# New waits for the late blocks' statistics and matmuls in the last search, and new preferences for the order of the queues

## The chip, the cores and the metric

The kernel runs on one core of a Trainium2 chip. The metric is the time of one execution on the device, in microseconds (us), and the number compared is the median of several runs.

## The reference

Two batches of 4096 tokens with 256 channels go through causal single-head attention and through a routed feed-forward layer. Each is followed by a residual sum and a normalisation. In the feed-forward layer the 3072 tokens of each batch with the highest router score get `x + gelu(x @ w_block)`. The others get `x + x`.

```python
x = _layernorm(x + attn(x, w_attn, b_attn, w_proj, b_proj))   # causal softmax(q k^T / 16) v, then w_proj
scores = jnp.einsum('bld,d->bl', x, w_router)
_, top_idx = jax.lax.top_k(scores, k)                          # k = 3072 of 4096, per batch
selected = jnp.take_along_axis(x, top_idx[:, :, None], axis=1)
processed = jax.nn.gelu(jnp.einsum('bkd,de->bke', selected, w_block))
out = x.at[batch_idx, top_idx].set(processed)
x = _layernorm(x + out)
```

## The kernel before, in words

**Groups.** The 8192 queries are cut into 16 groups of 512, eight for each batch (G = 0 to 15). For a group the kernel first projects queries and values. It casts a block of the transposed x to its high part (`xhi`, ScalarE, L747) and subtracts that for the low part (`xlo`, GpSimd, L765). TensorE then makes two query halves in bank fbank, which `qhi` (ScalarE, L792) and `qlo` (VectorE, L797) turn into high and low parts. The values are made in the same way (`vhi`, L826, and `vlo`, L830), and SyncE stores them in DRAM (L841). From there they are loaded again for every group that needs them, into six buffers (L1019).

**Attention.** Scores are matmuls into sbank (line L515 of the helper `split3`), tile by tile, 128 keys by 512 queries. ScalarE copies them to a ring (L872), VectorE keeps a running maximum, subtracts it (L982), ScalarE takes the exponential and a high part (L989, L996), VectorE the low part (L1001), and TensorE multiplies with the values (L1049 to L1051). The output is normalised, the router score is taken, and the feed-forward part follows: a transposition (L1340), matmuls, gelu (L1392), a sum on GpSimd (L1404), statistics `bn_stats` on VectorE (L1410) and their means `bn_aggr` (L1415). GpSimd makes the final scale factors from those (`final_roots`).

**Two late groups.** The feed-forward part of groups 14 and 15 (`LATE` is 14) is done after the last attention matmul, in single-pass matmuls (L1374), one piece for each half group j and 128-token tile.

**The search.** Which tokens are left out follows from a search for the 3072nd highest score. It has eight rounds (`ROUNDS` is 4, two halves of the key). In each round VectorE compares all keys with 15 thresholds (L1503, in two pieces for the second batch), TensorE counts the hits (L1559), and VectorE reduces the counts and decides (L1514, L1520). Between the counts TensorE gets fillers without use for the result (L555). After the last round come the ties (L1526, L1527, L1575, L1577) and the selection (L1534 to L1539). For the second batch, VectorE then picks one of two ready outcomes for 256 tokens at a time (L1752, 16 picks), and SyncE stores each pick (L1715).

**What sets the order.** The order of every queue is computed before the program is built. Each piece of work belongs to a named stream of an engine. The planner (`planned`, called by `merged`) rehearses all streams with costs of its own and takes for each engine the piece that can start first. `MARGIN_US` makes a stream's pieces look later, and `PREFER_US` lets them win where several could start. Among pieces that could start at one time the longest remaining way decides, to which the preference is added. Waits that a piece carries count in the rehearsal, so an added wait moves its piece. Each engine then works strictly in that order. On the chip a piece waits at its turn for its semaphores, and all that stands behind it in its queue waits too.

The semaphores of the change are `p_last` (counts of the second search done, by TensorE), `v_cmp` (compares done), `v_sel` (tie masks made) and `v_tie` (tie positions made), all three by VectorE.

Of the kernel before, what the change touches and what calls it, by code (L numbers as in the profile page):

```python
# [17 lines left out]
B, T, C = 2, 4096, 256  # L18
# [3 lines left out]
QT = GQ // P  # L22
# [12 lines left out]
ROUNDS = 4  # L35
# [7 lines left out]
LATE = 2 * (T // GQ) - 2  # L43
# [9 lines left out]
COLD_US, COLD, COLD_STREAMS = 4.0, 1.85, ()  # L53
TABLE_US = 1.28

PREFER_US = {"ffn flo": 100, "final load": 100, "project vhi": 100, "ffn store": 100, "last chain": 60,
             "last router": 60, "project qhi": 60, "attention_out residual": 60, "project qlo": 60,
             "attention_out stats": 60, "ffn fhi": 60, "attention_out score": 60, "row_max": 60,
             "final store": 60, "search first": 60, "scores copy": 30, "softmax hi": 30, "final pick": 30,
             "search": 30, "ffn stats": 15, "values load": 15, "prepare xlo": 8, "attention_out norm": 8,  # L60
             "row_max reduce": 4, "project xhi": 4, "project vlo": 4, "softmax lo": 4, "ffn gelu": 4,
             "project load": 4, "attention_out evac": 4, "prepare bias": 4, "scores hide": -4, "softmax exp": -4,
             "softmax z": -4, "final result": -4, "ffn add": -4, "ffn aggr": -8, "attention_out router": -8,
             "attention_out aggr": -8, "attention_out istd": -8, "last": -8, "final scale": -15, "final own": -15,
             "final choose": -30, "prepare": -30}
MARGIN_US = {"attention_out router": 3, "final scale": 3, "project xhi": 2, "ffn flo": 2, "final_roots": 2,
             "prepare bias": 1.5, "out": 1.5, "ffn store": 1.5, "scores hide": 1, "values load": 0.6,
             "ffn aggr": 0.6, "row_max reduce": 0.6, "values": 0.6, "project load": 0.3, "proj": 0.3,
             "attention_out stats": 0.3}

COSTS = {"pe": (.0, 1 / 2400, .2), "act": (.13, 1 / 1200, .14), "dve": (.09, 1 / 960, .12),
# [208 lines left out]
def program(nc, x, xt, w_attn_t, columns, w_proj, b_proj, w_router, w_block, out):  # L280

    gid = lambda b, g: b * NG + g
    groups = [(b, g) for b in range(B) for g in range(NG)]
# [39 lines left out]
    for f in out_fills:  # L323
        kind, G, j = f
# [4 lines left out]
    for f in late_fills:  # L329
        kind, G, j = f  # L330
# [12 lines left out]
    with ctx:  # L343
# [59 lines left out]
        score = sb("score", [P, B, NT])  # L403
# [42 lines left out]
        p_s, p_proj, p_out, p_last, p_late = sem("p_s"), sem("p_proj"), sem("p_out"), sem("p_last"), sem("p_late")  # L446
# [11 lines left out]
        v_cnt, v_tie, v_srch, v_cmp, v_sel = sem("v_cnt"), sem("v_tie"), sem("v_srch"), sem("v_cmp"), sem("v_sel")  # L458
# [12 lines left out]
        def bank_of(f):  # L471
            return (fbank + sbank + obank)[bank_no[f]]
# [85 lines left out]
        def late_busy(pe):  # L558

            pe.wait_ge(v_h, QT * len(groups))  # L560
            busy(pe, fbank[2][:, :], 2)
# [764 lines left out]
        def ffn(G):  # L1326

            b, g = groups[G]
            late = G >= LATE
# [27 lines left out]
                                  ALU.subtract).then_inc(v_flo, 1)  # L1357

            def pe_f(pe, j, tiles_=(0, 1)):
                if late and 0 in tiles_:  # L1360

                    pe.wait_ge(v_rs, 2 * len(groups) - 1)
                if late and 0 in tiles_:
                    pe.wait_ge(a_fhi, 2 * G + j + 1)
                    pe.wait_ge(ld_late, 16)
                    freed(pe, ("ff", G, j))
                elif 0 in tiles_:
                    pe.wait_ge(v_flo, 2 * G + j + 1)
                    if G == 0:
                        pe.wait_ge(v_wb, 2)  # L1370
                    freed(pe, ("ff", G, j))
                for t in tiles_ if late else ():
                    for k in range(CC):
                        mm = pe.matmul(bank_of(("ff", G, j))[:, t * C:(t + 1) * C],  # L1374
                                       x1p_of(G, j)[:, 0, k * 2 * P + t * P:k * 2 * P + (t + 1) * P], late_wb[:, k],
                                       start=k == 0, stop=k == CC - 1)
                for t in () if late else tiles_:
                    mm = split3(pe, bank_of(("ff", G, j))[:, t * C:(t + 1) * C],
                                lambda h, k: x1p_of(G, j)[:, h, k * 2 * P + t * P:k * 2 * P + (t + 1) * P],
                                lambda h, k: WB[:, h, k, :], CC)  # L1380
                if 1 in tiles_:
                    mm.then_inc(p_late if late else p_out, 1)
                    if G == LATE and j:
                        late_busy(pe)
# [14 lines left out]
            def add(pool, j):  # L1399
# [3 lines left out]
                    pool.wait_ge(v_sc, 2 * len(groups))  # L1403
                pool.tensor_tensor(y_pair(G, j), x1_pair(G, j), y_pair(G, j), ALU.add).then_inc(g_y, 1)  # L1404

            def stats(dve, t):
                dve.wait_ge(g_y, 2 * G + t // 2 + 1)
                if G and t == 0:
                    dve.wait_ge(v_mvy, QT * G)
                dve.bn_stats(bnst[:, 1, t, :], y_pair(G, t // 2)[:, t % 2]).then_inc(v_bny, 1)  # L1410

            def aggr(dve):
                for t in range(QT):
                    dve.wait_ge(v_bny, G * QT + t + 1)
                    dve.bn_aggr(mv_y[:, b, g * QT + t, :], bnst[:, 1, t, :]).then_inc(v_mvy, 1)  # L1415
# [475 lines left out]
```

## Time and profile before

| | |
|---|---|
| median of 3 runs | 969.17 us (966.97 to 973.5) |
| the profiled execution: its time | 968.08 us |
| the profiled execution: its span | 966.4 us |
| TensorE busy | 97% of the span |
| VectorE busy | 80% |
| ScalarE busy | 66% |
| mean granted clock of TensorE | 0.989 |
| last attention matmul (L1051) starts | 925.66 us |
| first pick starts | 951.42 us |

The times in the profile count from the span's start. The execution's own time is 1.68 us longer than the span. Line numbers are those of the kernel before.

### The profile page before, as it was taken

How to read it: one execution, taken by the hardware profiler on the slowest of the kernel's cores; microseconds unless marked ns; L12 is line 12 of the kernel's file. 1: busy time of each engine (PE TensorE's matmuls, PEld its weight loads, DVE VectorE, ACT ScalarE, POOL GpSimd, SP SyncE). 2: the span in 40 equal slices, each digit the busy share in tenths (PEclk: the TensorE clock that was granted, in tenths of full speed). 3: DMA queues.
4: the chain of work that ended last, by engine and by line, in shares of the span. 5: the costliest groups of instructions: out<-in, count | busy, mean ns of one | idle time of the engine just before them, and what ended most of it. 6: DMA issues, size and time to landing. Idle time of an engine off the chain costs nothing.

```text
span 966.4 us, 15640 instructions
## 1 busy us (share of the span) xinstructions
PE 939.0 (97%) x5078; PEld 805.6 (83%) x5078; DVE 769.3 (80%) x1473; ACT 635.3 (66%) x993; POOL 273.4 (28%) x436
## 2 busy tenths in 40 slices
PE   9999999999999999999999999999999999998991
PEld 7889988888888888888888999888888888887770
DVE  5688996967966786689769999887898778569977
ACT  3566675764864585478555875686688558447985
POOL 3523124253052034512214243323204302211162
PEclk9999999999999999999999999999999999999996
DMA  6535343344253345567433533535778534437935
GB/s 191 175 122 167 115 143 120 120 131 139 80 164 99 102 150 163 157 224 223 155 113 93 194 114 105 164 97 179 243 234 243 178 103 130 120 100 232 314 119 174
DMA packets 89378, 149.53 MB, mean 155 GB/s; under 512 B 7761, under 2 KB 25810, under 8 KB 89298
## 3 DMA queue, kind: packets, MB, share of 16 engines
q1 hardware_dynamic: 89298, 148.54, 48.9%
q8 instruction: 41, 0.67, 0.3%
q14 instruction: 39, 0.32, 0.1%
HBM read 108.66 MB, written 39.85 MB: 154 GB/s over the span
## 4 chain that ended last, share of the span: by engine, by line
PE 94%; DVE 3%; issue 1%; ACT 1%; POOL 0%; ACTq 0%; DVEq 0%; POOLq 0%
PE sbank L515 37%; PE fbank L515 13%; PE obank L1049 11%; PE obank L1051 11%; PE obank L1050 11%; PE obank L1043 2%; PE obank L1045 2%; PE obank L1044 2%; PE fbank L1340 1%; PE fbank L1139 1%; PE mbank L947 1%; PE mbank L970 1%; DVE cmp L1503 1%; PE obank L555 1%; ACT parts L996 0%
## 5 line engine op out<-in xcount | busy, mean ns | idle before, releaser
L515 PE MATMUL sbank<-qT,xT 128*128 128x512 f32 (+2 forms) x1728 | 413.2, 379 | 0.0
L515 PEld LDWEIGHTS sbank<-qT,xT 128*128 128x128 f32 x1728 | 306.4, 189 | 53.0 <-issue 0.3
L872 ACT COPY ring<-sbank 128x512 f32<-128x512 f32 (+3 forms) x288 | 157.6, 549 | 178.2 <-PE sbank L515 126.9
L1001 DVE TENSOR_TENSOR ring_lo<-ring,parts 128x1024 fp32r<-128x1024 f32 (+4 forms) x176 | 179.6, 1027 | 30.9 <-ACT parts L996 30.2
L1049 PE MATMUL obank<-ring_lo,vs 128*128 128x512 f32 x480 | 183.6, 383 | 4.3 <-ACT parts L996 2.6
L1051 PE MATMUL obank<-parts,vs 128*128 128x512 f32 x480 | 181.9, 379 | 0.0
L1050 PE MATMUL obank<-parts,vs 128*128 128x512 f32 x480 | 181.6, 378 | 0.0
L996 ACT CAST parts<-ring 128x1024 fp32r<-128x1024 f32 (+4 forms) x176 | 145.9, 834 | 51.7 <-PE obank L1051 38.9
L982 DVE TENSOR_TENSOR ring<-ring,mbank 128x1024 f32<-128x1024 f32 (+4 forms) x176 | 159.4, 946 | 9.4 <-PE mbank L970 9.4
L989 ACT ACTIVATE ring<-ring 128x1024 f32<-128x1024 f32 (+4 forms) x176 | 143.9, 844 | 24.7 <-DVE ring L982 24.4
L914 DVE TENSOR_TENSOR runmax<-ring,runmax 128x1024 f32<-128x1024 f32 x84 | 107.2, 1276 | 64.7 <-ACT ring L872 64.1
L1404 POOL TENSOR_TENSOR yb<-xres,yb 128x512 f32<-128x512 f32 x28 | 38.4, 1393 | 249.8 <-ACT yb L1392 249.8
L1049 PEld LDWEIGHTS obank<-ring_lo,vs 128*128 128x128 f32 x480 | 90.3, 188 | 20.8 <-ACT parts L996 3.3
L1051 PEld LDWEIGHTS obank<-parts,vs 128*128 128x128 f32 x480 | 90.2, 188 | 17.0
L1050 PEld LDWEIGHTS obank<-parts,vs 128*128 128x128 f32 x480 | 90.4, 188 | 15.9
L1100 POOL TENSOR_TENSOR xres<-xres,b_tot 128x512 f32<-128x512 f32 x32 | 50.9, 1610 | 66.9 <-DMA xres<-x 65.6
L909 DVE TENSOR_TENSOR runmax<-ring,runmax 128x512 f32<-128x512 f32 (+3 forms) x76 | 42.6, 561 | 15.6 <-ACT ring L872 14.2
L765 POOL TENSOR_TENSOR xT<-xraw,xT 128x512 fp32r<-128x512 f32 x27 | 35.2, 1324 | 66.9 <-ACT xT L747 65.9
L1070 POOL TENSOR_SCALAR roots<-mv_h 128x4 f32<-128x4 f32 x15 | 5.3, 357 | 163.2 <-DVE mv_h L1168 148.5
L515 PE MATMUL fbank<-WV,xT 128*128 128x256 f32 x384 | 51.1, 283 | 0.0
L515 PEld LDWEIGHTS fbank<-WV,xT 128*128 128x128 f32 x384 | 49.5, 191 | 1.7
L515 PE MATMUL fbank<-xT,A 128*128 128x512 f32 x192 | 49.3, 393 | 1.6 <-DVE qT L797 0.8
(222 smaller groups left out, 1203.6 us busy)
## 6 DMA issues: line engine op xcount, KB each, us to landing
vs<-v_scratch SPq DMA_DIRECT2D x288, 256.0 KB, 2.8
v_scratch<-vnew SPq DMA_DIRECT2D x30, 512.0 KB, 3.2
xres<-x SPq DMA_DIRECT2D x16, 512.0 KB, 4.6
out<-tail SPq DMA_DIRECT2D x32, 256.0 KB, 3.2
x_scratch<-xres SPq DMA_DIRECT2D x14, 512.0 KB, 3.0
y_scratch<-yb SPq DMA_DIRECT2D x14, 512.0 KB, 4.6
tail<-x_scratch SPq DMA_DIRECT2D x28, 256.0 KB, 3.5
tail<-y_scratch SPq DMA_DIRECT2D x28, 256.0 KB, 4.3
```

The costliest lines, as they stand in the source:

```text
L515: mm = eng.matmul(o, lhs(lh, k), rhs(rh, k), start=n == 0, stop=n == len(todo) - 1)
L872: act.copy(slot(n)[:, c0:], sbank[n % NSS][:, c0:]).then_inc(a_copy, 1)
L909: dve.tensor_tensor(runmax[:, 0, c0:], slot(n)[:, c0:], runmax[:, 0, c0:], ALU.max).then_inc(v_max, 1)
L914: dve.tensor_tensor(runmax[:, :, :], slots(ns, 0), runmax[:, :, :], ALU.max).then_inc(v_max, 1)
L982: dve.tensor_tensor(slots(ns, c0), slots(ns, c0), mbank[:, None, c0:].broadcast_to([P, len(ns), GQ - c0]), ALU.subtract).then_inc(v_z, 1)
L989: act.activation(slots(ns, c0), slots(ns, c0), ACT.Exp, scale=SCALE).then_inc(a_exp, 1)
L996: act.copy(hi_of(u), slots(ns, c0)).then_inc(a_hi, 1)
L1001: dve.tensor_tensor(slots_lo(ns, c0), slots(ns, c0), f32(hi_of(u)), ALU.subtract).then_inc(v_lo, 1)
L1049: pe.matmul(o, vh, lo_, start=i == 0, stop=False)
L1050: pe.matmul(o, vh, hi_, start=False, stop=False)
L1051: mm = pe.matmul(o, vl, hi_, start=False, stop=last)
L1100: pool.tensor_tensor(r[:, 2 * j:2 * j + 2], r[:, 2 * j:2 * j + 2], b_tot[:, None, :].broadcast_to([P, 2, C]), ALU.add).then_inc(g_xres, 1)
```

## The change

It has three parts.

1. The tables `PREFER_US` and `MARGIN_US` have other entries: `project vhi` (100), `final pick` (60) and `softmax exp` (-4) go, `attention_out store` (30) comes, `project xhi` goes from 4 to 15 and loses its margin of 2, `search first` goes from 60 to 30, and a few more.
2. Each late matmul piece of group 15 (`pe_f`) waits for a number of counts: 2 for half 0 tile 0, then 3, 4 and 5.
3. Each statistic of groups 14 and 15, and the means of each, gets a place in the search by a wait (`late_turn`). The numbers n run from 0 to 4 for group 14 and from 5 to 9 for group 15. Up to 6 the wait is for the compares of a round, 7 waits for the tie masks, and 8 and 9 wait for the tie positions.

```diff
+             "values load": 15, "project xhi": 15, "prepare xlo": 8, "attention_out norm": 8, "ffn gelu": 8,
...
             def pe_f(pe, j, tiles_=(0, 1)):
+                if G == len(groups) - 1:
+
+                    pe.wait_ge(p_last, 2 + 2 * j + tiles_[0])
                 if late and 0 in tiles_:
...
+            def late_turn(dve, t):
+
+                n = (G - LATE) * (QT + 1) + t
+                if n < 2 * ROUNDS - 1:
+                    dve.wait_ge(v_cmp, 2 * ROUNDS + 2 * (n + 2))
+                elif n == 2 * ROUNDS - 1:
+                    dve.wait_ge(v_sel, 2 * B)
+                else:
+                    dve.wait_ge(v_tie, B)
+
             def stats(dve, t):
                 dve.wait_ge(g_y, 2 * G + t // 2 + 1)
+                if late:
+                    late_turn(dve, t)
...
             def aggr(dve):
+                if late:
+                    late_turn(dve, QT)
```

The order of all five queues follows from this anew. The tables of the order below show three places. Names are those of the tiles, with the buffer's number; the words in brackets are the semaphores that an instruction waits for. In the order of the change the lines have other numbers (L746 is L747 of before, L791 is L792).

ScalarE at the start, before: two casts of the first x block, the two query halves, then two casts of the next x blocks.

```order
L750 CAST xT<-xraw 128x512 [waits ld_xh0]
L750 CAST xT<-xraw 128x512 [waits ld_xh1]
L792 ACTIVATE qT<-fbank0,ucol 128x512 [waits v_u,p_proj]
L792 ACTIVATE qT<-fbank1,ucol 128x512 [waits v_u,p_proj]
L747 CAST xT<-ring 128x2x512 [waits ld_xt0_1]
L747 CAST xT<-ring 128x2x512 [waits ld_xt0_2]
```

The same place with the change:

```order
L749 CAST xT<-xraw 128x512 [waits ld_xh0]
L749 CAST xT<-xraw 128x512 [waits ld_xh1]
L791 ACTIVATE qT<-fbank0,ucol 128x512 [waits v_u,p_proj]
L746 CAST xT<-ring 128x2x512 [waits ld_xt0_1]
L791 ACTIVATE qT<-fbank1,ucol 128x512 [waits v_u,p_proj]
L746 CAST xT<-ring 128x2x512 [waits ld_xt0_2]
```

The first of the two casts now stands between the two query halves.

TensorE in the third and fourth round of the last search, before (cmp is what is counted, obank0 takes group 15's late matmuls, fbank2 the fillers):

```order
L1374 MATMUL obank0<-runmax,late_x 128x256 [waits ld_late,a_fhi,v_rs]
L1374 MATMUL obank0<-runmax,late_x 128x256
L1559 MATMUL fbank0<-cmp,ones_bf 128x120 [waits v_cnt,v_cmp]
L1559 MATMUL fbank0<-cmp,ones_bf 128x120
L1374 MATMUL obank0<-runmax,late_x 128x256 x2
L1559 MATMUL fbank0<-cmp,ones_bf 128x120 [waits v_cmp]
L1559 MATMUL fbank0<-cmp,ones_bf 128x120
L555 MATMUL fbank2<-ones_bf 128x512 [waits v_h]
L555 MATMUL fbank2<-ones_bf 128x512
L1340 MATMUL obank1<-ident,tail 128x128 [waits v_ot,v_ow,p_last,a_x1]
```

The same place with the change (L1376 is L1374 of before, L1575 is L1559):

```order
L1376 MATMUL obank0<-runmax,late_x 128x256 [waits ld_late,a_fhi,v_rs,p_last]
L1376 MATMUL obank0<-runmax,late_x 128x256
L1575 MATMUL fbank0<-cmp,ones_bf 128x120 [waits v_cnt,v_cmp]
L1575 MATMUL fbank0<-cmp,ones_bf 128x120
L1575 MATMUL fbank0<-cmp,ones_bf 128x120 [waits v_cmp]
L1575 MATMUL fbank0<-cmp,ones_bf 128x120
L554 MATMUL fbank2<-ones_bf 128x512 [waits v_h]
L554 MATMUL fbank2<-ones_bf 128x512
L1376 MATMUL obank0<-runmax,late_x 128x256 [waits p_last]
L1376 MATMUL obank0<-runmax,late_x 128x256
L1339 MATMUL obank1<-ident,tail 128x128 [waits v_ot,v_ow,p_last,a_x1]
```

The second pair of late matmuls has moved from between the count's two pieces to behind the count and its filler. The last four (sbank0) are parted in the same way: two stay ahead of the fifth count, and two go ahead of the sixth.

VectorE from the last decision of the search to the end, before:

```order
L1526 TENSOR_SCALAR gteq<-mbank,tab 128x32 [waits v_srch]
L1527 TENSOR_SCALAR gteq<-mbank,tab 128x32
L1415 BN_AGGR mv_y<-bnst 128x2 [waits v_bny] x4
L1534 SCALAR_TENSOR_TENSOR keyf<-ones,fbank 128x64 [waits p_last]
L1535 TENSOR_TENSOR keyf<-keyf,fbank 128x32 [waits v_srch]
L1537 SCALAR_TENSOR_TENSOR keyf<-keyf,gteq 128x32 [waits v_tie]
L1539 SCALAR_TENSOR_TENSOR mbank<-keyf,gteq 128x32 [waits v_srch]
L1752 COPY_PREDICATED tail<-mbank,tail 128x512 [waits a_own,a_sums,v_srch]
L1752 COPY_PREDICATED tail<-mbank,tail 128x512 [waits a_sums,a_own,v_srch] x15
```

The same place with the change:

```order
L1542 TENSOR_SCALAR gteq<-mbank,tab 128x32 [waits v_srch]
L1543 TENSOR_SCALAR gteq<-mbank,tab 128x32
L1424 BN_STATS bnst<-tail 128x6 [waits v_sel,g_y]
L1550 SCALAR_TENSOR_TENSOR keyf<-ones,fbank 128x64 [waits p_last]
L1551 TENSOR_TENSOR keyf<-keyf,fbank 128x32 [waits v_srch]
L1553 SCALAR_TENSOR_TENSOR keyf<-keyf,gteq 128x32 [waits v_tie]
L1555 SCALAR_TENSOR_TENSOR mbank<-keyf,gteq 128x32 [waits v_srch]
L1424 BN_STATS bnst<-tail 128x6 [waits v_tie,g_y,v_srch]
L1768 COPY_PREDICATED tail<-mbank,tail 128x512 [waits a_sums,a_own,v_srch] x5
L1431 BN_AGGR mv_y<-bnst 128x2 [waits v_bny,v_tie]
L1431 BN_AGGR mv_y<-bnst 128x2 [waits v_bny] x3
L1768 COPY_PREDICATED tail<-mbank,tail 128x512 [waits a_sums,a_own,v_srch] x11
```

Two statistics now stand behind the search's last compare, and the means stand behind the fifth pick. In the rounds before, the statistics are one after the third compare, two after the fourth, one after the fifth, the means after the sixth, and one each after the seventh and eighth. Before they are two after the third and two after the fourth, the means and one after the fifth, one after the sixth, none after the seventh and two after the eighth.

## Rows read from the trace of the kernel before

**Rows 1.** The page, part 1: busy us, share of the span and instructions.

```profile
PE 939.0 (97%) x5078; PEld 805.6 (83%) x5078; DVE 769.3 (80%) x1473; ACT 635.3 (66%) x993; POOL 273.4 (28%) x436
```

**Rows 2.** TensorE's waits, whole span: who waited for whom, us in total, times, longest.

```profile
PE obank L1049 <- ACT parts L996: 2.6, 2, 1.4
...
PE fbank L515 <- DVE qT L797: 0.8, 1, 0.8
```

**Rows 3.** Busy us of PE, PEld, DVE, ACT, POOL; PE clock, DMA share, GB/s.

```profile
500.00:600.00 100.00, 99.71 (x654) 90.90 (x653) 92.62 (x221) 70.27 (x118) 37.94 (x69) 1.00 0.42 134
```

**Rows 4.** Timeline, 0 to 36 us: start, us, engine, line, out<-in, idle time before.

```profile
11.93 0.69 ACT L792 ACTIVATE qT<-fbank,ucol 128x512 fp32r<-128x512 f32 x1 [0.67 <-PE fbank L515]
12.65 0.75 DVE L797 SCALAR_TENSOR_TENSOR qT<-fbank,ucol,qT 128x512 fp32r<-128x512 f32 x1 [0.61 <-ACT qT L792]
...
13.31 0.42 DVE L692 CAST WB<-ring 128x512 fp32r<-128x512 f32 x1
...
14.68 1.05 ACT L747 CAST xT<-ring 128x1024 fp32r<-128x1024 f32 x1 [2.07 <-DMA ring<-xt]
...
15.80 2.70 POOL L765 TENSOR_TENSOR xT<-ring,xT 128x512 fp32r<-128x512 f32 x2 [8.01 <-ACT xT L747]
15.81 1.55 DVE L677 CAST WV<-ring 128x512 fp32r<-128x512 f32 x1
...
16.37 4.26 PE L515 MATMUL sbank<-qT,xT 128*128 128x512 f32 x12
17.40 1.65 DVE L681 TENSOR_TENSOR WV<-ring,WV 128x512 fp32r<-128x512 f32 x1
...
20.47 3.04 PE L515 MATMUL fbank<-WV,xT 128*128 128x256 f32 x24
```

**Rows 5.** Busy time in single microseconds at the start, columns as in rows 3.

```profile
16.00:17.00 1.00, 1.00 (x4) 0.63 (x4) 1.00 (x1) 0.95 (x1) 1.00 (x1) 0.85 1.09 352
...
20.00:21.00 1.00, 1.00 (x9) 1.00 (x8) 0.43 (x1) 0.33 (x1) 0.00 (x0) 0.94 0.08 16
```

**Rows 6.** The chain that ended last, 920 us on: start, us, what.

```profile
936.78 0.43 PE fbank L555 x2
937.22 0.86 PE obank L1374 x4
938.18 0.92 PE obank L1374 x4
939.25 0.30 DVE mbank L1514
...
940.64 0.66 DVE bnst L1410 x2
...
945.35 0.30 DVE mbank L1514
...
947.11 0.30 DVE mbank L1514
...
948.50 0.66 DVE bnst L1410 x2
...
950.01 0.29 DVE mv_y L1415 x4
```

**Rows 7.** Timeline of the end, and the busy time of one microsecond of it.

```profile
951.42 9.85 DVE L1752 COPY_PREDICATED tail<-mbank,tail 128x512 f32<-128x512 uint32 x16
...
953.38 2.08 ACT L1742 ACTIVATE tail<-tail,fin 128x256 f32<-128x256 f32 x4 [1.47 <-POOL fin L1643]
...
964.00:965.00 1.00, 0.00 (x0) 0.00 (x0) 0.00 (x0) 0.00 (x0) 0.00 (x0) 0.50 1.02 348
```

**Rows 8.** SyncE's waits, and the page's part 6 on value loads.

```profile
SPq L1019 <- PE obank L1051: 431.5, 197, 7.9
...
SPq L841 <- DVE vnew L830: 65.0, 23, 10.9
...
vs<-v_scratch SPq DMA_DIRECT2D x288, 256.0 KB, 2.8
```

More of the change, by code:

```diff
@@ L54 @@
 TABLE_US = 1.28
[L56 to L65, printed above, removed]
@@ L66 @@
-MARGIN_US = {"attention_out router": 3, "final scale": 3, "project xhi": 2, "ffn flo": 2, "final_roots": 2,
+PREFER_US = {"ffn flo": 100, "final load": 100, "ffn store": 100, "last chain": 60, "last router": 60,
+             "project qhi": 60, "attention_out residual": 60, "project qlo": 60, "attention_out stats": 60,
+             "ffn fhi": 60, "attention_out score": 60, "row_max": 60, "final store": 60, "scores copy": 30,
+             "softmax hi": 30, "search": 30, "search first": 30, "attention_out store": 30, "ffn stats": 15,
+             "values load": 15, "project xhi": 15, "prepare xlo": 8, "attention_out norm": 8, "ffn gelu": 8,
+             "row_max reduce": 4, "project vlo": 4, "softmax lo": 4, "project load": 4, "attention_out evac": 4,
+             "prepare bias": 4, "scores hide": -4, "softmax z": -4, "final result": -4, "ffn add": -4,
+             "attention_out router": -8, "attention_out aggr": -8, "attention_out istd": -8, "last": -8,
+             "final scale": -15, "final own": -15, "final_roots own": -15, "final choose": -30, "prepare": -30}
@@ L67 @@
+MARGIN_US = {"attention_out router": 3, "final scale": 3, "last": 3, "ffn flo": 2, "final_roots": 2,
              "prepare bias": 1.5, "out": 1.5, "ffn store": 1.5, "scores hide": 1, "values load": 0.6,
-             "ffn aggr": 0.6, "row_max reduce": 0.6, "values": 0.6, "project load": 0.3, "proj": 0.3,
+             "row_max reduce": 0.6, "values": 0.6, "ffn aggr": 0.3, "project load": 0.3, "proj": 0.3,
              "attention_out stats": 0.3}
```

## The prediction

> **What bounds the kernel now.** I read the page's busy times first: TensorE is busy 939.0 of 966.4 us [rows 1]. What it waited for in the whole span comes next: softmax parts 2.6 us, a query's low part 0.8 us, and less than that for each of the rest but three [rows 2]. So until the last block TensorE decides alone, and a change of order on the other engines is worth at most those waits, or costs what it adds to them. The middle is where the others are fullest: VectorE is busy 92.62 us of 500 to 600, TensorE still 99.71 [rows 3]. Two places are different. At the start all engines are strung on one chain of loads, casts and matmuls [rows 4, 5]. At the end TensorE's array is nearly idle, the chain goes through VectorE's compares, counts and statistics [rows 6], and then through 16 picks and 16 stores [rows 7].
>
> The profiled execution took 968.08 us, 1.68 more than its span, and lies 1.09 under the median of the runs shown, 969.17. I make the sum against 968.08 and add 1.09 for the median.
>
> **Start: ScalarE's cast of the second x block before the second query half.** The changed tables put this cast (L747) ahead of the second query evacuation (L792). Before, that evacuation starts at 11.93 and takes 0.69, VectorE's low part follows at 12.65, and the cast starts at 14.68, after 2.07 us of waiting for its load [rows 4]. The load's own start hangs on other loads alone, so its landing should not move. ScalarE works in order: it will stand at the cast until 14.68, end it at 15.73, and evacuate the query half by 16.42. VectorE's low part takes 0.75: to 17.20. The first scores need it. They now start at 16.37 (16.44 on the chain), right behind other matmuls; they will start at 17.25, and that is +0.8 us of idle TensorE that nothing hides.
>
> Queued behind that low part on VectorE are the casts of the block's weights (from 13.31) and all of the value weights (15.81 to 19.05) [rows 4]. 17.13 takes the place of 13.31, so the value weights' cast comes 3.8 us later, at 19.6, with one 0.15 us column moved ahead of it at 19.8. Those two instructions take 1.55 and 1.65 now, beside GpSimd's subtraction, which runs from 15.80 to 18.50. The same form of cast at 13.31, with GpSimd idle, took 0.42. By 19.8 GpSimd is done, so I count 0.42 and, for the low part, the 0.75 of the query's: ready at 20.9. But now the cast that began at 13.31 starts inside GpSimd's 15.80 to 18.50, and pays the difference of 1.55 and 0.42: ready at 22.0. The scores themselves run 4.1 us, mostly at the lower clock, so they end at about 21.4. The value projection, which starts at 20.47 now, waits for the later of both. Bounds: +0.8 (only the scores count) and +1.5 (VectorE's chain). I take +1.4, since the cast meets the very GpSimd instruction that the 1.55 us row met.
>
> The clock in this stretch: 0.85 granted from 16 to 17 and 0.94 from 20 to 21 [rows 5], so the lower level, 1.2 GHz, from about 16.7 to 20.1; before it fell TensorE was busy all the time. I let the low stretch move with the scores.
>
> Two rules speak here. The Trainium skill, "SBUF — State Buffer", "Who interferes with whom", makes the port that VectorE shares with GpSimd an exclusive lock, held for a whole instruction. By it the cast at 17.13 does nothing until 18.50 and ends at 18.92, and the start costs 1.6 instead of 1.4. The Trainium skill, "TensorE: Matmul & The Clock Gate", Part 1, says that the monitor behind the clock runs free and is not set off by the program. By it the clock could return at 20.1 all the same, the scores would end 0.2 us earlier, and the sum stays, as VectorE's chain is later.
>
> **Body: orders of all engines re-dealt.** Some forty single matmul groups change places on TensorE, and ScalarE's and VectorE's orders differ in the first 130 us, at 345 to 450 and at 470 to 720. From about 830 to 930 no engine's order differs, so the waits there (the 2.6 of [rows 2] among them) stay. Of the moved places only two show a TensorE wait of now: 0.8 for a query's low part at 422 and 0.3 for a running maximum at 523. Gain at most 1.1. On the other side, moves of one or two ScalarE instructions (about 1 us each) where VectorE is 93% busy [rows 3] can open new waits of 0.3 to 1.5 us, as the existing ones are. I take 0, and keep -1.1 and +3.
>
> **Last block: search, late matmuls, statistics.** A round of the search that nothing disturbs takes 1.76 us from one count's reduce to the next (945.35 to 947.11) [rows 6].
> - Third count: two late matmul groups of 0.86 and 0.92 stand around its first piece, and its reduce comes at 939.25, 2.43 after the one before. The change puts the second of them behind the whole count: 0.67 earlier.
> - Fourth count: that group, the transposes and two fillers (0.43 each) now stand ahead of it. From 938.5: 0.43 + 0.9 + 0.45 + 0.43 and the count's 0.35 give a reduce at 941.05. Now it comes at 941.2, held by two statistics (0.66). So 0.5 of the 0.67 is given back; 0.15 stays.
> - Fifth: means (0.29, as for the ties) and one statistic (0.33, half of a pair) after the compare become one statistic, and only half of the eight late matmuls is ahead of the count: 0.35 earlier.
> - Sixth and seventh: means or one statistic (0.3 to 0.4) fit under the count, which takes that long after the compare: 0.
> - Eighth: two statistics (0.66, ending at 949.16) become one; the reduce comes 2.0 after 947.11 instead of 1.76: 0.2 earlier.
> - Ties: a statistic instead of the means (0.29) under TensorE's two matmuls: 0.
> - The new waits on v_cmp, v_sel and v_tie are for instructions that VectorE itself has just ended. Each costs the overlap of two neighbours, under 0.1 us, and lies under the count: 0. What stands behind them is the next reduce.
> - The last statistic comes after the selection and before the first pick: 0.4 later.
> Together the first pick moves by -0.7 + 0.4 = -0.3 us, to 951.1.
>
> The picks take 9.85 us for 16, the transfers of 4.19 MB at 348 GB/s take 12.1 [rows 7], so the transfers end the kernel and start with the first pick. The means between the fifth and the sixth pick (0.37) are hidden: after five picks the transfers are 0.7 us behind, and at the end 2.3 us. The last two picks now need, after the means, GpSimd's roots (950.30 to 953.38, 3.1 us) and four ScalarE scalings (2.08) [rows 7]: 951.1 + 5 x 0.62 + 0.4 + 5.1 = 959.7, and the last pick starts at 960.8. The cover is 1.1 us thick here and 2.3 more in the transfers. If the means come over 3 us late, this is the new end. Term: -0.3; bounds -0.8 (the fourth count keeps its gain) and +0.4 (the rounds give nothing).
>
> **Sum.** 968.08 + 1.4 + 0 - 0.3 = 969.2, and 970.3 for the median.
>
> **Rivals.**
> 1. *The rounds give nothing.* If counts are paced by TensorE's late groups in every round, the first pick comes 0.1 to 0.4 later. For it: the fourth count already is. Against: the sixth to eighth have no late group. 968.08 + 1.4 + 0.4 + 1.09 = 971.0. Chance 0.18.
> 2. *Faster.* The x block lands before 12.6 when nothing else waits for it, or the clock's low stretch shrinks, so the start costs nothing; the waits at 422 and 523 go (-1.1); the tail gives 0.8. 968.08 - 1.9 + 1.09 = 967.3. Against: the load's landing is read at 14.68 and its chain of loads is not touched. Chance 0.15.
> 3. *Slower: the value projection loses its preference (100 to 0).* Six of its casts on ScalarE come later (at 346.7 it is passed by about seven instructions, to some 12 us later), then VectorE's part, then the store, and the SyncE queue is in order: the loads of value tiles stand behind that store. For it: the queue already stands 65.0 us for these parts [rows 8]. Against: the loads wait 431.5 us for free buffers, up to 7.9 at a time, and TensorE never for a load [rows 2, 8]. It decides from where a store comes more than the six buffered tiles (8 to 16 us) late; each such place costs up to a landing of 2.8 us [rows 8]. One or two places: +3, 973.3; all six: +17. Chance 0.20, of which 0.04 for over 9.7 us.
> That a wait added is already satisfied, and so changes nothing but the listed order, is part of the forecast: the order is what acts.
> The forecast itself has 0.47.
>
> **Range and chances.** Runs of one kernel spread over 966.97 to 973.5, so a median of a few can move by some 2 us. 966.6 takes in half of rival 2, 974.2 the common part of rival 3. A measurement here can tell about 1%, 9.7 us. Only the far end of rival 3 reaches that, and nothing on the other side but an error of mine: faster 0.02, within 0.94, slower 0.04.
>
> **What would show it.** In the new profile: ScalarE's cast at 14.7 ahead of the second query part, and the first scores at 17.2 (right) or 16.4 (wrong: rival 2). The value projection at 21.4 to 22.2. Reduces of the third and fourth count 1.8 and about 2.45 apart, the eighth 1.8 after the seventh. First pick about 0.3 earlier counted from the last value matmul, five picks, the means, eleven picks without a gap, DMA share at 1.0 to the end. New TensorE waits for value loads would mean rival 3. A difference of over 3 us with none of these would make the whole reading wrong.

## The result and the profile after

The changed kernel takes 974.08 us (median of 13 runs, 971.37 to 976.11), the one before 969.17 (13 runs, 966.97 to 973.5): a ratio of 1.0044, with an interval of 1.0032 to 1.0057. It is slower by some 4 us. The number lies inside the range (966.6 to 974.2) by 0.1 us, and within the 1% that I called the same. The forecast was 1.1 us more, not 4, and the upper end of the range stood for rival 3, which did not happen. So the hit of the range is luck.

The profiled execution has a span of 970.7 us, 4.3 more than before. Lines have moved: L746 is L747 of before, L791 L792, L796 L797, L871 L872, L1424 L1410, L1431 L1415, L1530 L1514, L1768 L1752. Its page, part 1, against [rows 1]:

```profile
PE 940.1 (97%) x5078; PEld 805.5 (83%) x5078; DVE 772.9 (80%) x1473; ACT 634.4 (65%) x993; POOL 275.2 (28%) x436
```

TensorE has 1.1 us more of work and 4.3 us more of span, so most of the loss is waiting. Its waits (us in total, times, longest) against [rows 2]:

```profile
PE obank L1048 <- ACT parts L995: 3.1, 2, 1.7
...
PE mbank L946 <- DVE runmax L908: 1.2, 2, 0.9
PE sbank L514 <- ACT ring L871: 1.2, 1, 1.2
...
PE fbank L514 <- DVE qT L796: 0.8, 1, 0.8
```

Two are new against that profile, 1.2 on the ring's copy and 0.95 on the running maximum. (The second turns up in traces of the old order too, see below.) The wait of 0.8 at the query's low part is still there: a gain at the places that I had allowed to go did not come.

**The start** (start, us, engine, line, out<-in, idle before), against [rows 4]:

```profile
14.56 1.04 ACT L746 CAST xT<-ring 128x1024 fp32r<-128x1024 f32 x1 [3.15 <-DMA ring<-xt]
...
15.51 0.68 ACT L791 ACTIVATE qT<-fbank,ucol 128x512 fp32r<-128x512 f32 x1
15.68 2.76 POOL L764 TENSOR_TENSOR xT<-ring,xT 128x512 fp32r<-128x512 f32 x2 [7.91 <-ACT xT L746]
...
16.23 0.75 DVE L796 SCALAR_TENSOR_TENSOR qT<-fbank,ucol,qT 128x512 fp32r<-128x512 f32 x1 [4.03 <-ACT qT L791]
16.89 0.41 DVE L691 CAST WB<-ring 128x512 fp32r<-128x512 f32 x1
...
17.08 4.21 PE L514 MATMUL sbank<-qT,xT 128*128 128x512 f32 x12 [0.48 <-issue]
17.34 1.65 DVE L693 TENSOR_TENSOR WB<-ring,WB 128x512 fp32r<-128x512 f32 x1
...
20.34 0.43 DVE L676 CAST WV<-ring 128x512 fp32r<-128x512 f32 x1
20.80 0.69 DVE L680 TENSOR_TENSOR WV<-ring,WV 128x512 fp32r<-128x512 f32 x1
...
21.55 0.62 PE L514 MATMUL fbank<-WV,xT 128*128 128x256 f32 x3 [0.27 <-DVE WV L680]
```

The cast stands ahead of the query half, waits for its load and delays the first scores to 17.08 (17.2 was forecast). VectorE's chain of weights ends last, and the value projection starts at 21.55 instead of 20.47. The clock of that stretch, against [rows 5]:

```profile
16.00:17.00 1.00, 0.60 (x2) 0.19 (x2) 0.77 (x2) 1.00 (x2) 1.00 (x2) 1.00 1.09 356
17.00:18.00 1.00, 0.92 (x2) 0.83 (x3) 0.97 (x2) 0.13 (x1) 1.00 (x1) 0.50 1.10 363
20.00:21.00 1.00, 1.00 (x6) 0.96 (x5) 0.93 (x5) 0.59 (x1) 0.00 (x0) 0.79 0.00 0
```

It fell to 1.2 GHz, as in the profile of before, here at the moment when the scores began.

**Where the 4.3 us arise.** Matched by the number of the value matmul, TensorE is behind by 1.08 us from the value projection to 355 us, by 2.46 at 407, by 3.62 at 574 and by 4.27 at 906. After that nothing is lost: the first pick starts 25.86 us after the last attention matmul (25.76 before). The four steps are 1.08, 1.38, 1.16 and 0.6 us. The second is this one, first before (VectorE's means and ScalarE, 399 to 406 us), then after:

```profile
399.10 0.37 DVE L1168 BATCH_NORM_AGGREGATE mv_h<-bnst 128x2 f32<-128x6 f32 x4
402.89 0.59 ACT L872 COPY ring<-sbank 128x512 f32<-128x512 f32 x1 [0.24 <-PE obank L1051]
404.43 1.59 ACT L1250 ACTIVATE xres<-xres,rstd,rs_h 128x256 f32<-128x256 f32 x3 [0.96 <-POOL rstd L1209]
```

```profile
401.19 0.37 DVE L1167 BATCH_NORM_AGGREGATE mv_h<-bnst 128x2 f32<-128x6 f32 x4
401.65 1.05 ACT L995 CAST parts<-ring 128x1024 fp32r<-128x1024 f32 x1
406.57 0.60 ACT L1249 ACTIVATE xres<-xres,rstd,rs_h 128x256 f32<-128x256 f32 x1 [3.86 <-POOL rstd L1208]
407.07 0.56 ACT L871 COPY ring<-sbank 128x512 f32<-128x512 f32 x1
407.69 1.65 PE L514 MATMUL sbank<-qT,xT 128*128 128x512 f32 x6 [1.18 <-ACT ring L871]
```

The new order puts a normalisation ahead of a copy. The normalisation waits 3.86 us for GpSimd's factor, the copy waits behind it, and the scores wait 1.18 us for the bank that the copy frees. VectorE's new order has a part in it: the means from which GpSimd makes that factor start at 401.19 instead of 399.10, 2.1 us later, where TensorE was only 1.0 behind. Near 570 us, the third step, GpSimd's final factors stand ahead of the roots that the normalisations need, and the copies stand behind these:

```profile
570.07 1.09 ACT L1249 ACTIVATE xres<-xres,rstd,rs_h 128x256 f32<-128x256 f32 x2 [1.73 <-POOL rstd L1208]
```

This order is not the whole cause there: three traces of the old order (the waits alone, the end by hand, the new end alone) have a wait of 0.85 to 1.10 us on the same running maximum. The fourth step is a load of x that landed after 6.0 instead of 5.5 us.

**The end** (VectorE), against [rows 6] and the picks of [rows 7]:

```profile
950.91 0.27 DVE L1530 TENSOR_REDUCE mbank<-fbank 128x15 f32<-128x120 f32 x1
...
951.44 0.84 DVE L1519 SCALAR_TENSOR_TENSOR cmp<-mbank,tab,jtab 128x240 bf16<-128x240 f32 x2
952.74 0.43 DVE L1424 BATCH_NORM_STATS2 bnst<-tail 128x6 f32<-128x256 f32 x1 [0.46 <-DVE cmp L1519]
953.08 0.27 DVE L1530 TENSOR_REDUCE mbank<-fbank 128x15 f32<-128x120 f32 x1
...
955.79 3.14 DVE L1768 COPY_PREDICATED tail<-mbank,tail 128x512 f32<-128x512 uint32 x5
958.83 0.36 DVE L1431 BATCH_NORM_AGGREGATE mv_y<-bnst 128x2 f32<-128x6 f32 x4
```

From one reduce to the next, third to eighth: 1.76, 2.37, 2.13, 1.75, 1.81, 2.17 us, and 2.71 to the first pick. Before: 2.43, 1.96, 2.40, 1.74, 1.76, 1.97 and 2.34. In the eighth round VectorE stands idle for 0.46 us between the compare that it has ended and the statistic that waits for this very compare. The picks then run as forecast, and the transfers last to the end as in the last row of [rows 7]:

```profile
968.00:969.00 1.00, 0.00 (x0) 0.00 (x0) 0.00 (x0) 0.00 (x0) 0.00 (x0) 0.50 1.02 341
```

### The profile page after: what moved, and what is told of

The parts are those of the page before. It is cut to its first block, busy times and chain, and to the rows that moved or that the text cites. A ratio compares the mean times of both kernels' runs of the same rounds, so it can differ in the third digit from the quotient of the medians.

```text
span 970.7 us, 15647 instructions
## 1 busy us (share of the span) xinstructions
PE 940.1 (97%) x5078; PEld 805.5 (83%) x5078; DVE 772.9 (80%) x1473; ACT 634.4 (65%) x993; POOL 275.2 (28%) x436
## 4 chain that ended last, share of the span: by engine, by line
PE 81%; DVE 6%; POOL 4%; issue 4%; DMA 3%; ACT 2%; DVEq 0%; SPq 0%; ACTq 0%; POOLq 0%
PE sbank L514 32%; PE fbank L514 12%; PE obank L1048 10%; PE obank L1050 10%; PE obank L1049 10%; DMA xraw<-xt 2%; PE obank L1042 1%; PE obank L1044 1%; PE obank L1043 1%; POOL xT L764 1%; PE fbank L1339 1%; PE mbank L946 1%; PE fbank L1138 1%; PE mbank L969 1%; DVE ring L981 1%
## 5 line engine op out<-in xcount | busy, mean ns | idle before, releaser
L871 ACT COPY ring<-sbank 128x512 f32<-128x512 f32 (+3 forms) x288 | 157.5, 548 | 172.1 <-PE sbank L514 126.6
L1000 DVE TENSOR_TENSOR ring_lo<-ring,parts 128x1024 fp32r<-128x1024 f32 (+4 forms) x176 | 181.6, 1040 | 27.5 <-ACT parts L995 26.3
L913 DVE TENSOR_TENSOR runmax<-ring,runmax 128x1024 f32<-128x1024 f32 x84 | 110.4, 1315 | 66.4 <-ACT ring L871 65.7
L764 POOL TENSOR_TENSOR xT<-xraw,xT 128x512 fp32r<-128x512 f32 x27 | 40.0, 1501 | 56.9 <-ACT xT L746 56.0
```

Of the source, the lines that this page charges most:

```text
L764: pool.tensor_tensor(xT[:, 1, k, cols], raw_of(G)[:, k, :], f32(xT[:, 0, k, cols]), ALU.subtract).then_inc(g_xlo, 1)
L871: act.copy(slot(n)[:, c0:], sbank[n % NSS][:, c0:]).then_inc(a_copy, 1)
L913: dve.tensor_tensor(runmax[:, :, :], slots(ns, 0), runmax[:, :, :], ALU.max).then_inc(v_max, 1)
L1000: dve.tensor_tensor(slots_lo(ns, c0), slots(ns, c0), f32(hi_of(u)), ALU.subtract).then_inc(v_lo, 1)
```

## The experiments

Theory A held that the places of the new order in the start and the body cost the 4 us, theory B that the waits in the search do. Theory C came up on the way: the wait near 570 us differs from one execution to the next, and not by the order. So did theory D: the swap at the start costs much because TensorE stands idle ahead of the first scores and its clock then falls. Orders were put together by overwriting stretches of the planned lists of streams, such as:

```diff
     orders, times = planned(todo, signalled, urgency(todo))
+    for e, at, names in PLACED:
+        orders[e][at:at + len(names)] = names
```

Ratios are to the kernel before, which ran again beside each group of experiments: 29 runs with a median of 970.1 for the first four, 26 with 968.3 for the next four, 32 with 969.38 for the last four. Single traces of one order differ by up to 2 us at the start alone, so I read places from traces and sums from ratios.

### The waits alone, with the old tables

```diff
-PREFER_US, MARGIN_US = (the new tables)
+PREFER_US, MARGIN_US = (the old tables)
```

> The kernel with the change, but with the old tables of preferences and margins: only the waits of the late statistics and of group 15's late matmuls are left. Theory A (the cost comes from three places of the new order: start 1.1 us, near 407 us 1.4, near 572 us 1.2): the last attention matmul starts within 0.3 us of where it does before (925.66), the first pick follows it by 25.8 to 25.9 us instead of 25.76, and the time is 968.7 to 969.7 where before has 969.2, a ratio of 1.000 to 1.001. Theory B (the waits in the search cost it, and the steps before it are scatter of one profiled execution): the ratio stays at 1.004. The eighth count's reduce comes 2.17 us after the seventh, as with the change, if the 0.46 us that VectorE stood ahead of that round's statistic belongs to the order, and 1.8 if it was scatter.

972.2 us, ratio 1.0018 (1.0003 to 1.0034), more than A expected and less than B. The body shows no new wait but one of 0.85 near 567 us. In the trace the eighth reduce comes after 1.96 us, neither of the two values expected, and the first pick after 25.30, but the means stand behind the 14th pick:

```profile
958.45 0.34 DVE L1420 BATCH_NORM_AGGREGATE mv_y<-bnst 128x2 f32<-128x6 f32 x4
963.09 0.73 DVE L1757 COPY_PREDICATED tail<-mbank,tail 128x512 f32<-128x512 uint32 x1 [4.30 <-ACT tail L1747]
```

The 15th pick waits 4.30 us for GpSimd's factors and ScalarE's scaling. From the first pick to the end of the span it takes 17.8 us instead of 14.9. This is the cover that the prediction measured (1.1 us, and 2.3 more in the transfers), broken by means that stand 8.9 us behind the first pick, where the change has 3.0. The old tables do it. Which entry was not tried: they have `final pick` at 30 (the description ahead of the prediction gives 60, a slip) and `ffn aggr`, the means, at -8.

### The tables alone

```diff
-PREFER_US, MARGIN_US = (the old tables)
+PREFER_US, MARGIN_US = (the new tables)
```

The base is the kernel before.

> The kernel before with the new tables and without the new waits. Theory A: the last attention matmul starts 4.0 to 4.4 us later than before (at about 929.9), and the time is 4 us longer, a ratio of 1.0035 to 1.0055. Theory B: a ratio within 0.001 of 1. Waits of TensorE of 1.2 near 407 and 0.95 near 572 us appear by A, none by B.

976.58 us, ratio 1.0067 (1.0046 to 1.0088), worse than both parts together. The waits near 407 (1.10) and 575 us (1.23) are there. Two costs come on top in the trace. The load of the second block landed later, so the first scores started at 18.86. In the other 13 traces it landed by 15.4, so I put that down to this execution and not to the tables. And without the new waits the new tables crowd late matmuls into the second and third rounds of the search, with reduces 3.60 and 3.66 us apart. From the first reduce to the first pick it takes 18.92 us (before 16.36, change 16.46). The two halves of the change need each other at the end.

### The changed kernel with the old neighbours at the start

```diff
+PLACED = [('act', 3, [('project qhi', 1), ('project xhi', 2)])]
```

> The kernel with the change, its order kept but for two neighbours on ScalarE: the second query half goes ahead of the cast of the second x block again. Theory A: first scores at 16.4 to 16.5 us instead of 17.1, the value projection at 20.5 instead of 21.55, every later step 1.1 us earlier, time 1.0 to 1.1 less than with the change (about 973.0, ratio to before 1.0033). Rival (the value projection waits for VectorE's casts beside GpSimd in any case, or a later stage takes the gain back): less than 0.3 us less.

971.32 us, ratio 1.0014 (1.0000 to 1.0028), about 3 us less than the change measured, not 1.1: theory A has the place right and the size wrong. The first scores start at 15.99 and the value projection at 18.55 us. The clock did not fall in this trace.

### The changed kernel with the old order at three places

```diff
+PLACED = (the old lists of act from 3 to 5, 346 to 373 and 528 to 542,
+          of dve from 406 to 414 and 618 to 628, of pool from 57 to 60 and 89 to 91)
```

> The kernel with the change, with the old order of ScalarE, VectorE and GpSimd at the three places where TensorE lost time (start, 339 to 373 in ScalarE's list, that is near 400 us, and near 560 us); all other places keep the new order. Theory A: the waits near 407 and 572 us are gone, the last attention matmul starts 3.4 to 3.7 us earlier than with the change, time about 970.4, ratio to before 1.0005 to 1.0015. Rival (any re-dealing costs, since the engines are full: a place put back opens a wait elsewhere): ratio stays above 1.003.

973.03 us, ratio 1.0032 (1.0013 to 1.0052): as the rival had it. The wait near 407 is gone, but one of 2.45 us stands at 577.9, where three lists were the old ones and TensorE's the new one. A place is an arrangement of all queues. Put back in part, it is a third arrangement.

### The end by hand

```diff
-PE:  late, count 3a, late, count 3b, transposes, count 4, late, late, count 5
+PE:  late, count 3, late, count 4, transposes, count 5, late, count 6, late, count 7
-DVE: count 8, ties, means, selection, picks 1 to 16
+DVE: count 8, ties, a statistic, selection, picks 1 to 3, last statistic, picks 4 and 5, means, picks 6 to 16
```

The base is the kernel before. The statistics of the rounds ahead stand as with the change.

> The kernel before, without new waits and with its old tables; only the order from the last search on is set by hand. The late matmul groups stand one per count (after the second to the sixth decision, the transposes in a round of their own), the statistics stand as with the change except that the last one comes behind the third pick instead of ahead of the first, and the means stay behind the fifth pick. If TensorE's late groups and one statistic per round set the pace, as the prediction's steps say: the reduces of the third to the seventh count follow at 1.76, 2.05, 1.78, 1.75 and 1.78 us, the first pick comes 24.8 us after the last attention matmul instead of 25.76 (before) and 25.86 (with the change), and the time is 0.9 less than before, a ratio of 0.999. Rival (what a round saves comes back at the picks or as a later wait): the first pick still 25.4 or more after, or gaps between picks, ratio 1.000 or more.

968.67 us, ratio 1.0000 (0.9984 to 1.0016). From the first reduce to the first pick it takes 15.17 us instead of 16.36 (before) and 16.46 (change), with the third to the sixth reduce after 1.76, 1.96, 2.04 and 1.76. The last statistic behind the third pick gives back 0.2 in the transfers (15.2 from the first pick to the end, before 14.9). The gain of some 1 us in the trace is below what the runs tell apart. It is the fastest end tried, and not shown to beat the kernel before.

### The three places in the kernel before

```diff
+PLACED = (the same stretches, in the new order, and of pe from 472 to 479)
```

> The kernel before with only the order of the change put in at three places: the two neighbours on ScalarE at the start; the lists of ScalarE, VectorE and GpSimd near 400 us; those and TensorE's near 560 us. Theory A: the start costs 1.1, the place near 407 us 1.4 and the place near 572 us 1.2, together 3.5 to 3.7, ratio 1.0037. Theory C (the kernel with the waits alone showed a wait of 0.85 at 567.6 us with the old order, so the third place differs from one execution to the next and not by the order): 2.5, ratio 1.0025, and a wait near 407 but none or one of another size near 572.

981.68 us, ratio 1.0135 (1.0105 to 1.0165): neither theory. The stretch near 400 us cost 5 us, with a wait of 2.55 at 395.95 that no whole order has. Behind it TensorE's clock was at the lower level until 400 us, so a part of the 5 us is the clock:

```profile
397.00:399.00 2.00, 2.00 (x6) 1.57 (x5) 2.00 (x2) 0.33 (x1) 1.99 (x1) 0.50 0.00 0
```

It is the flaw of the three-places kernel again, larger, and says nothing of the change. The start alone and the two stretches of all five queues, below, do it cleanly.

### The start alone

```diff
+PLACED = [('act', 3, [('project xhi', 2), ('project qhi', 1)])]
```

> The kernel before with only ScalarE's cast of the second x block ahead of the second query half. The prediction's start step: first scores at 17.1 to 17.3 us and the value projection at 21.5 us where TensorE's clock is low in that stretch, time 1.0 to 1.4 more than before, ratio 1.0011 to 1.0014. Rival (the cast's load lands at other times in other executions, up to 3 us later): 2 us and more. Rival (a later wait takes it up, or the load is early): under 0.4.

973.11 us, ratio 1.0042 (1.0023 to 1.0060): two neighbours on one engine cost as much as the whole change. The trace has the value projection at 21.88 us.

### The new end alone, without waits

```diff
+PLACED = (the new lists of dve from 1036, pe from 775, act from 894 and pool from 130, to their ends)
```

> The kernel before, without the new waits, with exactly the order that the change has from the last search on (all of VectorE, TensorE, ScalarE and GpSimd there). If only the order acts and the waits are satisfied when their turn comes: reduces at 1.76, 1.76, 2.37, 2.13, 1.75, then 1.76 to 1.81 us, and the first pick 25.3 to 25.9 us after the last attention matmul; the time is the one of before within 0.3 us. If the 0.46 us that VectorE stands in the eighth round comes from the wait for the compare that it has just issued, it is gone here and the eighth reduce follows after 1.8 instead of 2.17, the first pick after 25.5. If it stays, it is the place in the order or in the program.

968.18 us, ratio 0.9998 (0.9976 to 1.0020). The same place in the trace:

```profile
947.49 0.29 DVE L1525 TENSOR_REDUCE mbank<-fbank 128x15 f32<-128x120 f32 x1
...
948.04 0.84 DVE L1514 SCALAR_TENSOR_TENSOR cmp<-mbank,tab,jtab 128x240 bf16<-128x240 f32 x2
948.80 0.42 DVE L1421 BATCH_NORM_STATS2 bnst<-tail 128x6 f32<-128x256 f32 x1
949.25 0.29 DVE L1525 TENSOR_REDUCE mbank<-fbank 128x15 f32<-128x120 f32 x1
```

The same order without the waits: the statistic begins under the compare, and the eighth reduce follows after 1.76 us. From the first reduce to the first pick it takes 15.84 us, with the waits 16.46 (16.46, 16.46, 16.48 and 16.47 in four traces). So by the traces the order gains 0.5 and the waits cost 0.6. The runs cannot tell either from nothing.

### The start with its idle time filled

```diff
+                if n == 0 and not isinstance(pe, Rehearsal):
+                    busy(pe, sbank[1][:, :], 6)
```

The base is the kernel of the start alone, with its swap of two neighbours. The fillers (`busy`, six matmuls) are hidden from the planner, so that no order changes.

> The kernel before with ScalarE's cast of the second x block ahead of the second query half, as in the run of that swap alone, and with six filler matmuls without use (128x512, some 0.22 us each, 1.3 us together) into a free bank just ahead of the first scores, all orders kept. Theory D (the swap costs so much because TensorE stands idle ahead of the first scores, 0.5 to 3.2 us in four traces, and its clock then falls to 1.2 GHz in all four, where it fell in two of six traces of the old order; a fall costs 1.7 us of the 2.6 that the scores take at 2.4 GHz): with the idle time filled the clock stays at 1.00 through the scores, the value projection starts at 19.6 to 20.3 us instead of 21.9, and the time is 1.5 us less than with the swap alone, ratio to before 1.001 to 1.002; executions with a mean clock of 0.990 or more, none of nine with the swap alone, are a third or more. Rival (the clock falls there whether TensorE idles or not, the cost is the late load alone): the scores take 4.2 us again and the ratio stays at 1.004.

972.68 us, ratio 1.0031 (1.0013 to 1.0049). TensorE's rows and the clock at 18 us:

```profile
17.89 2.69 PE L523 MATMUL sbank<-qT,xT 128*128 128x512 f32 x12 [0.59 <-issue]
22.38 2.90 PE L523 MATMUL fbank<-WV,xT 128*128 128x256 f32 x22 [1.80 <-DVE WV L689]
```

```profile
18.00:19.00 1.00, 1.00 (x5) 0.82 (x6) 0.97 (x2) 0.00 (x0) 1.00 (x1) 1.00 0.94 328
```

Theory D is half right. The clock stayed up, and the scores took 2.69 us instead of 4.2. Five of 12 executions have a mean clock of 0.990 or more, none of nine with the swap alone. (A fall at any place lowers this mean, so it counts falls roughly, and not those of the start alone.) But the value projection now waits 1.80 us for VectorE's weights and starts at 22.38. VectorE's chain bounds the start, with or without the clock. The load landed late in this trace (15.37, with the swap alone 14.89). The runs do not tell this kernel from the start alone (1.0042).

### The new order from 345 to 450 us, and from 520 to 720 us

```diff
+PLACED = (the new lists of act from 323 to 402, dve 380 to 448, pool 57 to 60, sp 140 to 182, pe 290 to 292)
```

> The kernel before with the whole new order of all five queues between about 345 and 450 us, and the old one everywhere else. If the wait near 407 us belongs to the new order (it stood in the traces of all three kernels with the whole new order of the body and in none of the five with the old one): a wait of 1.1 to 1.2 there, 1.4 us of shift behind it, ratio 1.0014. Rival (the sum of small places): no wait over 0.3 there and a ratio of 1.000.

970.41 us, ratio 1.0012 (0.9999 to 1.0025). The wait is there, and TensorE is 1.4 us further behind after it. The interval of the runs just includes 1:

```profile
406.48 0.73 PE L527 MATMUL sbank<-qT,xT 128*128 128x512 f32 x2 [1.10 <-ACT ring L884]
```

```diff
+PLACED = (the new lists of act from 501 to 624, dve 618 to 761, pool 89 to 91, sp 229 to 279, pe 472 to 535)
```

> The kernel before with the whole new order of all five queues between about 520 and 720 us, and the old one everywhere else. The wait near 570 us was there in three of five traces with the old order (0.85 to 1.10) and in all three with the new one (0.94 to 1.23). If it is a matter of chance in both: 0 to 0.5 us more on average, ratio 1.0000 to 1.0005. If the new order makes it certain and adds the small ones at 521 and 525: 1.0 or more, ratio 1.001 and up.

969.85 us, ratio 1.0002 (0.9987 to 1.0018), with a wait of 0.90 at 567.8: the middle of it is near nothing. All traces with the new order there lose 1.1 to 2.6 us between 520 and 580. Those with the old one lose nothing (before, the start alone) or 1.0 to 1.5.

### The changed kernel once more

No edit.

> The changed kernel once more, beside the parts of its order above. Theory D with the other parts: the time is the sum of the start (2.5 to 3), the place near 407 us (1.4), 0 to 0.5 near 570 us, and the end (0.1), 4.0 to 5.0 over before, ratio 1.004 to 1.005; the first scores start at 17 us or later, the clock falls with them, and no more than one execution in ten has a mean clock of 0.990 or more. Rival (one of the parts was scatter of single traces): under 3 us.

973.9 us (9 runs), ratio 1.0048 (1.0026 to 1.0069), as the sum of the parts had it.

## Why the prediction was right or wrong

**Start: mechanism right, size wrong, 1.4 forecast and about 3 measured.** The first scores came at 17.08 and the value projection at 21.55, by VectorE's chain and not by the scores, as worked out. Two durations inside that chain were off. The cast beside GpSimd's instructions took 0.41 and not 1.55, and the subtraction behind it took 1.65 and not some 0.7. That the two nearly cancel is luck. The larger fault is the step's base, "the clock in this stretch: 0.85 granted from 16 to 17", taken as what the kernel does. It is what one execution did. In the eight traces with the old start, the profile of before among them, the value projection starts at 20.47, 20.46 and 20.36 us in three where the clock fell, and at 18.23, 18.33, 18.55, 18.61 and 19.05 in five where it did not. Mean 19.3. One of the five (the new end alone):

```profile
16.49 2.72 PE L526 MATMUL sbank<-qT,xT 128*128 128x512 f32 x12
19.05 3.03 PE L526 MATMUL fbank<-WV,xT 128*128 128x256 f32 x24
```

With the new start it is 21.55, 21.78, 21.88, 22.27 and 23.47: mean 22.2, since VectorE's chain hides the clock and is itself late with the load. The difference is 2.9 us, and it agrees with the 4.1 (2.2 to 5.8) of the start alone. A part of the 4.1 may be later falls of the clock: near 885 us it fell in four of the five traces with the new start and in three of the eight with the old, at 1.6 us each. Whether the start changes that chance stays open. The comparison of the two profiled executions shows only 1.08 of the 2.9, as both had the low clock. The bound of +1.5 was too narrow.

**Body: 0 forecast, some 1.5 to 2.5 measured.** "I take 0, and keep -1.1 and +3": of that, the lower half was empty. The wait near 407 us is in all five traces with the whole new order there, and costs 1.32 to 1.41; in none with the old one. By the runs of that stretch alone it is 1.2 (-0.1 to 2.4). The place near 570 adds 0.2 by the runs (-1.3 to 1.7). The traces suggest up to 1, and that stays open. Theory C is thus right in part: the wait comes with the old order as well. The place near 407 us is what the step named, one ScalarE instruction moved past another, and VectorE's later means with it. I did not follow such moves one by one, though the order showed the normalisation ahead of the copy and the trace showed that its factor comes late. The 0.6 at 906 us is not the change's. The wait there runs from 0.65 to 2.24 us in 14 traces of either order.

**End: -0.3 forecast, +0.1 measured.** Third count -0.67 (forecast the same), fourth +0.41 (+0.5), fifth -0.27 (-0.35), sixth and seventh +0.06 (0), last statistic and ties +0.37 (+0.4). The eighth was to be 0.2 earlier and is 0.2 later. The step that failed is the sentence that the new waits cost 0. Without them the same order gains 0.5 in its one trace, with them it loses 0.1 in four. The means behind the fifth pick were hidden, and the kernel with the waits alone shows the cover's edge.

**Rivals.** TensorE waited for no value load, so rival 3 did not happen. Rival 1 (the rounds give nothing, 971.0) is true in its effect, by another cause. The 4 us came from the start at twice its forecast size and from the body that was put at 0.

**The sum now.** 2.9 + 1.4 + 0.2 to 1 + 0.1 is 4.6 to 5.4 us, against 4.3 (3.1 to 5.5) and 4.65 (2.5 to 6.7) in the two comparisons.

## What to carry to other kernels

A sum made against one profiled execution inherits its luck. Where a stretch ran at the lower clock, ask what the step is worth when it does not, and keep both in the range. An instruction that waits for a load or a slow factor must not stand ahead of one that frees a bank: in an ordered queue look at each pair of neighbours that changes places, and ask which of them waits. A wait for an instruction just issued on the same engine need not be free: here one cost 0.46 us.

## What the hardware showed

- One program's granted clock differs between executions. With the old start it fell during the first scores in 3 of 8 traces. With the new start it fell in 5 of 5, ahead of the first scores or during them (at 17.0 to 18.1 us). Of 87 executions of the kernel before 39 had a mean clock of 0.990 or more, of 22 of the change 3, of nine with the start alone none. This fits the Trainium skill, "TensorE: Matmul & The Clock Gate", Part 1, by which the clock's monitor runs free. It can fall in mid-kernel too: in 7 of 14 traces, of either order, it fell after TensorE's two waits near 880 us (1.64 and 1.41 us long), and each such fall cost 1.6 us. In two more, the filled start and the changed kernel once more, it fell near 910 us. The start alone, 888 to 890 us:

```profile
888.00:890.00 2.00, 2.00 (x7) 1.54 (x6) 2.00 (x2) 1.98 (x3) 0.00 (x0) 0.50 0.70 263
```

- The load of the second x block was there for its cast at 14.29 to 16.34 us, a spread of 2 us. An order in which TensorE depends on it inherits that.
- GpSimd's subtraction slowed VectorE's subtraction (1.65 instead of 0.69) but not the cast at the border of its two instructions (0.41). By the Trainium skill, "SBUF — State Buffer", "Who interferes with whom", the port is locked exclusively. The subtraction agrees: it ended 0.5 us after GpSimd did. The cast settles nothing: it began at 16.89, and GpSimd's first instruction ended at 16.94 by a profile that is rough for GpSimd. Casts that began well inside that instruction do agree. In the profile of before one took 1.55, and in the new end alone one took 1.04. Both ended 0.3 us after it:

```profile
15.41 1.27 POOL L776 TENSOR_TENSOR xT<-ring,xT 128x512 fp32r<-128x512 f32 x1 [7.82 <-ACT xT L758]
15.93 1.04 DVE L688 CAST WV<-ring 128x512 fp32r<-128x512 f32 x1
```

- A statistic that waits for a compare just ended on its own engine started 0.46 us after it in one round, in four traces, and 0.1 in others. Why these differ was not tried.
